# A mixture-of-experts / attention kernel: the second stage's tokens are routed in four batches, most of them inside the attention

## The reference

```python
x = x + 0.5 * ffn(layernorm(x))
x = x + attn(layernorm(x), keys, values)     # 16 heads of 8, 512 keys; attn adds its own input
x = x + 0.5 * ffn(layernorm(x))
# ffn(z): xn = layernorm(z) * scale + bias; probs = softmax(xn @ gate.T)
#         the two best of 8 experts, their weights normalised to a sum of 1
#         out = swiglu(z; shared) + sum over the two of weight * swiglu(z; expert)
# swiglu: 128 -> 256 (gate, up) -> 128
```

## Time and profile before

| | us |
|---|---|
| median of 3 runs | 976.35 (974.88 to 979.6) |
| the profiled execution, its own time | 977.33 |
| its span, first to last instruction | 975.3 |
| first stage's routing, keys, scatters (0 to 129) | 129 |
| its 39 tiles (129 to 250) | 121 |
| results added (250 to 273) | 23 |
| attention with its start (273 to 701) | 428 |
| second stage: routing to its first tile (701 to 827) | 126 |
| its 39 tiles, results, stores (827 to 975.3) | 148 |

### The profile page before, as it was taken

How to read it: one execution, slowest core, us unless ns; L and a number is a source line. 1 busy time by engine, 2 the same in 40 slices (tenths; PEclk the granted TensorE clock), 3 DMA queues, 4 the chain that set the end, 5 groups by cost and what they waited for, 6 DMA issues and landing times.

```text
span 975.3 us, 13685 instructions
## 1 busy us (share of the span) xinstructions
PE 719.5 (74%) x4404; PEld 431.9 (44%) x4404; DVE 567.0 (58%) x1092; ACT 475.3 (49%) x733; POOL 530.2 (54%) x664
## 2 busy tenths in 40 slices
PE   4459669999026888888888888888645970999950
PEld 4325459999012333333333333333144540899950
DVE  5753324444327788888888888888348330444424
ACT  2232135555002677777777777777612210555530
POOL 5587726677151535464645464642175775466760
PEclk9859979999555799999999999999955995999985
DMA  8231123332400000000000000000000311333317
GB/s 235 84 97 59 60 75 98 91 96 64 151 22 0 1 7 19 7 19 7 20 7 19 7 19 8 19 7 20 14 11 32 107 61 63 88 91 91 99 54 232
DMA packets 57227, 55.09 MB, mean 56 GB/s; under 512 B 12828, under 2 KB 46367, under 8 KB 57158
## 3 DMA queue, kind: packets, MB, share of 16 engines
q1 hardware_dynamic: 48070, 36.38, 13.1%
q0 software_dynamic: 9088, 17.86, 5.1%
HBM read 29.13 MB, written 24.53 MB: 55 GB/s over the span
## 4 chain that ended last, share of the span: by engine, by line
PE 50%; POOL 19%; issue 9%; DVE 9%; ACT 7%; DMA 5%; SPq 1%; POOLq 0%; ACTq 0%; DVEq 0%
POOL slot_rows L1025 13%; PE psum L580 11%; PE psum L540 8%; PE psum L504 7%; PE psum L463 7%; PE psum L472 7%; ACT probs L687 6%; DVE neg_max L963 5%; PE psum L551 4%; PE psum L370 3%; DMA ycomb<-result_rows 3%; PE psum L396 1%; POOL a_z L1089 1%; POOL q_first L1098 1%; POOL rstd L1004 1%
## 5 line engine op out<-in xcount | busy, mean ns | idle before, releaser
L963 DVE TENSOR_REDUCE neg_max<-psum 128x1 f32<-128x512 f32 x512 | 329.0, 685 | 76.7 <-PE psum L551 68.0
L687 ACT ACTIVATE probs<-psum 128x1024 f32<-128x1024 f32 x256 | 255.7, 1024 | 80.7 <-PE psum L540 74.0
L918 DVE TENSOR_TENSOR work<-work,psum 128x512 f32<-128x512 f32 x110 | 74.4, 687 | 191.3 <-PE psum L472 133.3
L551 PE MATMUL psum<-k_stack,q_parts 32*128 32x512 f32 x512 | 133.8, 517 | 46.1 <-DVE neg_max L963 42.8
L1025 POOL DMA_INDIRECT slot_rows<-zrow,slot x128 | 127.3, 995 | 54.5 <-issue 45.8
L580 PE MATMUL psum<-probs,v_pad 128*32 128x512 f32 x1024 | 139.6, 618 | 0.2
L540 PE MATMUL psum<-q_full,k_stack 32*128 32x512 f32 x512 | 116.7, 479 | 17.6 <-ACT probs L687 17.6
L1044 POOL DMA_INDIRECT result_rows<-yrow,zslot x80 | 82.0, 1025 | 59.6 <-ACT yrow L661 30.2
L540 PEld LDWEIGHTS psum<-q_full,k_stack 32*128 32x128 f32 x512 | 48.2, 186 | 145.3 <-ACT probs L687 88.1
L648 ACT ACTIVATE work<-psum 128x512 f32<-128x512 f32 x110 | 65.7, 597 | 88.2 <-PE psum L457 66.3
L1044 POOL DMA_INDIRECT result_rows<-yrow,probs x76 | 77.1, 1014 | 30.0 <-issue 28.1
(11 more groups left out here) (160 smaller groups left out, 948.0 us busy)
## 6 DMA issues: line engine op xcount, KB each, us to landing
ycomb<-result_rows SPq DMA_DIRECT2D x32, 256.0 KB, 2.9
zslot<-slot_rows SPq DMA_DIRECT2D x40, 144.0 KB, 2.3
probs<-slot_rows SPq DMA_DIRECT2D x38, 144.0 KB, 2.3
slot_rows<-padrow SPq DMA_DIRECT2D x17, 144.0 KB, 1.9
x<-in_x SPq DMA_DIRECT2D x8, 256.0 KB, 4.0
slot_rows<-zrow,slot POOLq DMA_INDIRECT x128, 2.3
ycomb<-ycomb SPq DMA_DIRECT2D x64, 32.0 KB, 1.9
ycomb<-recip SPq DMA_DIRECT2D x32, 64.0 KB
```

Source lines behind the costliest of these rows:

```text
L551: mm(bank(M_BANK[m % 3]), q_parts[rows, u % 2, qt * P:(qt + 1) * P], k_stack[rows, u % HI, :], start=True, stop=True).then_inc(m_filled, 1)
L687: nc.scalar.activation(probs[:, k % PRING, 2 * jp:2 * jp + 2, :], psum[:, b:b + 2, :], ACT.Exp, scale=float(DH) ** -0.5).then_inc(s_freed, 1)
L918: tt(h[:, k % 2, :], silu[:, k % 2, :], bank(U_BANK[k % 2]), ALU.mult).then_inc(h_ready, 1)
L963: reduce(neg_max[:, u % 2, qt, j:j + 1], bank(M_BANK[m % 3]), AX.X, ALU.max, negate=True).then_inc(m_freed, 1)
```

## The change

- **Batches.** The first stage is routed in four batches of two groups, the second in batches of groups 0 to 3, 4 and 5, 6, and 7. Normalising moves from DVE to ACT (one ACTIVATE with a scale and a bias per tile, L764 goes). Logits and positions are copied from PSUM by ACT; their banks come from the attention's ring.
- **Second stage inside the attention.** Moments of group g are taken three steps after POST(g). For the first two batches, variance, deviations, normalising, transposes, logits, routing (one of its steps behind each M) and the scatters of 24 of the 32 tiles (one tile, two DMAs, per step) are put beside the steps; the scatters from step 93 on for the first batch, from step 123 on for the second.
- **Tail.** Groups 6 and 7 are routed and scattered between the groups of the shared expert, whose work now stands in the lists `first` and `second`. As `zT` the second stage uses free buffers, so SP waits for the last gate and up product before it loads a tile.
- **Results of the first stage.** Groups 0 and 1 are added ahead of the attention, group g+2 at step 12 of group g. `ycomb` lies in `zrow`, in pieces of 512 B. In the second stage loads and stores alternate.
- **PROJ.** ACT makes both `q_round` and `q_first` from PSUM; POOL only subtracts.
- **POOL.** Its set-up stands ahead of the first deviations; one power per batch in place of one per group.

```diff
-BG = 4
-NBATCH = NG // BG
-BT = BG * GT
+BATCHES = tuple((ph, groups) for ph, of in enumerate((((0, 1), (2, 3), (4, 5), (6, 7)), ((0, 1, 2, 3), (4, 5), (6,), (7,))))
+                for groups in of)
+PER_PHASE = len(BATCHES) // 2
+BT = 4 * GT
+NTT = NG * GT
 RT = 27
-TB = 15
+TB = 14
...
+        def zT_of(ph, g):
+
+            if ph == 0:
+                return zT[:, g, :]
+            if g < 4:
+                return w_now[:].rearrange("p a c -> p (a c)")[:, g * GTOK:(g + 1) * GTOK]
+            if g < 6:
+                return zslot[:].rearrange("p a b c -> p (a b c)")[:, (g - 4) * GTOK:(g - 3) * GTOK]
+            return zslot_T[:].rearrange("p a n -> p (a n)") if g == 6 else probs[:, 0, 0, :]
+
+        def ycomb(r, k):
+
+            at = NTT // 2 + (2 * (r % 2) + k) * GT
+            return zrow[:, 1, at:at + GT, 0:H]
...
+        def front(n):
+
+            return [("BV", n), ("BR", n), ("BZ", n)] + [("ZT",) + (BATCHES[n][0], g) for g in BATCHES[n][1]] + [("BD", n), ("LG", n)]
+
+        def moments(n):
+            return [("BM", BATCHES[n][0], g) for g in BATCHES[n][1]]
+
+        def routed(n, parts=(0, 1)):
+            return ([("R", n)] * 15 + [("EX", n), ("POS", n)] if 0 in parts else []) + ([("R", n)] * 12 if 1 in parts else [])
+
+        def scatters(n):
+            return [("SC", n, tau) for tau in range(tiles_of(n).start, tiles_of(n).stop)]
+
+        def shared(g):
+            return [("GU", 2 * g), ("GU", 2 * g + 1)] + ([("DS", g - 1)] if g else [])
+
+        first = moments(0) + front(0)[:2] + moments(1) + front(1)[:2] + front(0)[2:] + routed(0, (0,)) + moments(2) + front(2)[:2]
+        first += routed(0, (1,)) + scatters(0) + front(1)[2:] + routed(1, (0,)) + moments(3) + front(3)[:2] + routed(1, (1,)) + scatters(1)
+        for n in (2, 3):
+            first += front(n)[2:] + routed(n) + (scatters(n) if n == 2 else [])
+        first += [("CNT", 0), ("TAB", 0)] + scatters(3) + [("KEYS",)]
+        for g in range(NG):
+            first += shared(g)
+        first += [("DS", NG - 1)]
...
+        beside = {k: [] for k in range(NG * PER_GROUP)}
+        between = {k: [] for k in range(NG * PER_GROUP)}
+
+        def posted(g):
+            return PER_GROUP * (g + 1) + AT["POST"]
+
+        for g in range(NG - 1):
+            beside[posted(g) + 3].append(("BM", 1, g))
+        for n in (PER_PHASE, PER_PHASE + 1):
+            groups = BATCHES[n][1]
+            k0 = posted(groups[-1])
+            beside[k0 + 3] += [("BV", n)]
+            beside[k0 + 4] += [("BR", n)]
+            beside[k0 + 6] += [("BZ", n)]
+            for m, g in enumerate(groups):
+                beside[k0 + 7 + m].append(("ZT", 1, g))
+            k = k0 + 7 + len(groups)
+            beside[k] += [("BD", n), ("LG", n)]
+            for m in range(15):
+                between[k + 1 + m // 4].append(("R", n))
+            beside[k + 4] += [("EX", n), ("POS", n)]
+            for m in range(12):
+                between[k + 6 + m // 4].append(("R", n))
+            for m, ev in enumerate(scatters(n)):
+                beside[min(k + 9 + m, NG * PER_GROUP - 1)].append(ev)
...
+            m = []
+            for n, ev in enumerate(maxima(k + M_LEAD)):
+                m += [[ev] + between[k][n:n + 1]]
+            if not m:
+                m = [between[k], [], [], []]
+            out = [("S", k, 0)] + m[0] + m[1]
             out += [("AV", k - AV_LAG)] if k >= AV_LAG else []
             if k % (2 * KB) == AV_LAG - 1 and k > AV_LAG:
                 out += [("EVAC", k // (2 * KB) - 1)]
-            out += [("S", k, 1)] + m[2:]
+            out += [("S", k, 1)] + m[2] + m[3]
...
+            if r == AT["CB"] and g + 2 < NG:
+                out += [("CB", g + 2)]
...
+            return out + beside[k]
+
+        attention = [("CB", 0), ("MOM", 0), ("LN", 0), ("CB", 1), ("Z", 0), ("YT", 0), ("PROJ", 0), ("PROJ", 1)]
+        attention += maxima(0) + maxima(1) + maxima(2) + maxima(3) + [("MT", 0), ("PROJ", 2)] + maxima(4) + maxima(5)
+        attention += [e for k in range(NG * PER_GROUP) for e in step_events(k)]
+        attention += [("AV", NG * PER_GROUP - n) for n in range(AV_LAG, 0, -1)] + [("EVAC", 2 * NG - 1)]
+
+        m, n = len(BATCHES) - 2, len(BATCHES) - 1
+        second = front(m) + [("RECIP", NG - 1)] + shared(0) + routed(m, (0,)) + shared(1) + routed(m, (1,)) + [("POST", NG - 1)] + shared(2)
+        second += moments(n) + front(n) + shared(3) + scatters(m) + routed(n, (0,)) + [("CNT", 1)] + shared(4) + routed(n, (1,)) + [("TAB", 1)]
+        second += scatters(n)
+        for g in range(5, NG):
+            second += shared(g)
+        second += [("DS", NG - 1)]
+        events = first + attention + second
...
+                else:
+                    sp.wait_ge(up_ready, STEPS + 2 * NG)
...
+            def load_results(ph, g):
+                if g >= 2:
+                    sp.wait_ge(combined, ph * NG + g - 1)
+                for k in range(2):
+                    sp.dma_start(ycomb(g, k), d["yd"][(k * NG + g) * GTOK:(k * NG + g + 1) * GTOK].rearrange("(p t) f -> p t f", t=GT)
+                                 ).then_inc(comb_in[g % 2], 16)
...
+            for g in range(4):
+                load_results(0, g)
             for g in range(NG):
                 place(g)
-            sp.wait_ge(x_attended, NG)
+                if g + 4 < NG:
+                    load_results(0, g + 4)
             ffn(1)
+            for g in range(2):
+                load_results(1, g)
             for g in range(NG):
+                if g + 2 < NG:
+                    load_results(1, g + 2)
...
+            def logits(n):
+                ph, groups = BATCHES[n]
+                pe.wait_ge(s_freed, use_of["ZT", ph, groups[-1]] + 1)
+                b = claim(use_of["LG", n])
+                for m in range(len(groups) * GT):
+                    last = mm(psum[:, b, m * NE:(m + 1) * NE], zT_of(ph, groups[m // GT])[:, (m % GT) * P:(m % GT + 1) * P],
+                              gate_s[:, 0, :], start=True, stop=True)
+                last.then_inc(s_filled, 1)
...
+            def gate_up(ph, k):
+
+                g, i = divmod(k, 2)
+                if k == 0:
+                    pe.wait_ge(in_w[0], 48)
+                    if ph == 0:
+                        pe.wait_ge(v_ready, 1)
+                    else:
+                        pe.wait_ge(m_freed, len(max_of))
+                        pe.wait_ge(s_freed, use_of["S", NK - 1, 1] + 1)
+                if i == 0:
+                    pe.wait_ge(s_freed, use_of["ZT", ph, g] + 1)
+                if k >= 2:
+                    pe.wait_ge(silu_ready, ph * STEPS + k - 1)
...
+            def normalise(n):
+                ph, groups = BATCHES[n]
+                act.wait_ge(shift_done, n + 1)
+                if ph:
+                    act.wait_ge(dispatched, LANDED)
+                for g in groups:
+                    for t in range(GT):
+                        tau = g * GT + t
+                        last = nc.scalar.activation(zrow[:, 0, tau, 0:H], token_tile(x, tau), ACT.Identity,
+                                                    bias=shift[:, tau:tau + 1], scale=rstd[:, tau:tau + 1])
+                    last.then_inc(z_done, 1)
+
+            def double_z(n):
+                ph, groups = BATCHES[n]
+                act.wait_ge(z_done, ph * NG + groups[-1] + 1)
+                if ph and groups[-1] >= NG // 2:
+                    act.wait_ge(combined, NG)
+                nc.scalar.copy(zrow[:, 1, tiles_of(n), 0:H], zrow[:, 0, tiles_of(n), 0:H]).then_inc(z_doubled, 1)
...
-                        if u:
-                            act.wait_ge(q_ready, u)
-                        nc.scalar.activation(q_fp[:], bank(b), ACT.Relu, bias=bq[:, i:i + 1]).then_inc(s_freed, 1)
+                        if u >= 2:
+                            act.wait_ge(q_ready, u - 1)
+                        nc.scalar.activation(q_round[:, u % 2, :], bank(b), ACT.Relu, bias=bq[:, i:i + 1]).then_inc(q_rounded, 1)
+                        nc.scalar.activation(q_first[:, u % 2, :], bank(b), ACT.Relu, bias=bq_first[:, i:i + 1],
+                                             scale=first_row).then_inc(s_freed, 1)
...
+            def combine(ph, g):
+                xg = x[:, g, :].rearrange("p (t f) -> p t f", t=GT)
+                dve.wait_ge(comb_in[g % 2], (ph * (NG // 2) + g // 2 + 1) * 32)
+                if g == 0:
+                    dve.wait_ge(shared_added, (ph + 1) * NG)
+                tt(xg, xg, ycomb(g, 0), ALU.add).then_inc(comb_half, 1)
+                dve.wait_ge(comb_half, ph * NG + g + 1)
+                tt(xg, xg, ycomb(g, 1), ALU.add).then_inc(combined, 1)
...
+            scale_gates()
+            run_stage(0, first)
             ffn(0)
-            attend()
-            prepare(1)
+            run(attention)
+            run_stage(1, second)
             ffn(1)
+            for g in range(NG):
+                combine(1, g)
...
```

(42 more changed lines are left out.)

747 lines of the change are left out of this document (368 added, 379 removed).

## The result

The changed kernel takes 997.21 us (992.73 to 1013.29) against 976.59 (974.88 to 979.60): ratio 1.0179, 95% interval 1.0142 to 1.0217. Forecast were 967 and a range of 944 to 984. Its executions spread more than those of before. The ratio is that of the three shorter ones, and the profiled one is the longest, 1013.29, 16.1 us above the median. The same program profiled once more (first experiment) gave 1008.87 and the same picture; its median was 1000.82.

A forecast was written before the change was run, and what follows sets the result against it. No engine was taken to bound the whole: DVE and PE alternate in the attention, POOL bounds the seam before the tiles. Terms -18.4 + 45.3 - 41.6 + 5 - 0.5 = -10.2 on 977.33 gave 967 us, range 944 to 984.

The forecast's parts named there:

- Start of the attention: From the first stage to the attention: first moments 16.7 us earlier, 1.7 saved in PROJ; -18.4 us.
- First stage: Before the attention: POOL's later start and deviations behind scatters delay the first tile; +5 us, bounds 0 to 9.
- The attention: All attention groups: work added on DVE, PE, ACT and POOL, less a saved wait; +45.3 us, 5.7 per group.
- Additions and moments: DVE in the attention: six combinations of 8.4 us and seven moments of 5.6 us, charged at 83%.
- Routing steps: DVE in the attention: 54 routing operations, 11.3 us, charged at 83%.
- Normalising: ACT in the attention: 24 tiles in pieces of 5.8 and 2.9 us, PE and DVE going on for 1.5; 7.2 us.
- Scatters: POOL in the attention: tiles of two DMAs, 2.53 us each, exceed POOL's room; +6.5 us, bounds 0 to 25.
- The clock as a rival: Tail: PE stays at 1.2 GHz between pauses, half the shared expert's products cold, +14; 981 us, chance 0.12.
- The tail: From the attention's end to the second stage's first tile: 85 us (bounds 76 and 105) against 126.6; -41.6 us.
- The end: Second stage's stores issued between loads, saving most issues after the last addition; -0.5 us, bounds -4 and +4.
- nothing on balance: Shared expert waits for group 6 and becomes the tail; tail 90, attention 50, time 977 us; chance 0.12.
- POOL becomes the limit: Attention: scatters delay the maxima's stage, PE stands in MT, some 40 us show rather than 6.5; 988 us, chance 0.17.

The follow-up runs named there:

- first experiment: The changed kernel itself, run and profiled once more without any edit; median 1000.82 us, ratio 1.0227.
- run 7: Run 4's kernel with only the 24 tiles' scatters moved from the attention to the start of the tail; ratio 1.0043.
- run 15: Reordered tail and first stage, logits and dense routing of groups 0 to 3 inside the attention; their 16 tiles' scatters moved inside too; 952.88 us, ratio 0.9741.
- run 5: Run 4's kernel with two tiles normalised per step, row copies and logits one group at a time, positions one step later; ratio 0.9827.
- run 2: The kernel before plus ten extra bn_stats in one piece on DVE at the end of step 12 of each attention group; 998.65 us, ratio 1.0224.
- Run 4: The changed kernel with each addition of results in its own step and moments taken one tile at a time; 982.13 us, ratio 1.0066.
- Run 14: Reordered kernel with logits and routing of groups 0 to 3 inside the attention, one routing step per attention step instead of four; 963.21 us, ratio 0.9858.
- run 8: The program of run 6 repeated on a chip where the kernel before took 977.33 us; 973.83 us, ratio 0.9965.
- run 6: Run 4's kernel with all second-stage routing moved to the tail, only additions and moments left in the attention; ratio 0.9953.

## Why the prediction was wrong

- **Start of the attention, -18.4:** right. From the first tile to the moments it is 17.7 us less, against 16.7 worked out. Of the 1.7 for PROJ 0.5 shows: from the moments to the first product with `q_parts` 15.5 us instead of 16.0. (The 256 given as a sign left out the later start of +5 in the same forecast; it was 264.19.)
- **First stage, +5 (0 to 9):** right in kind, but 9.7 is over the bound. The keys begin at 70.83 against 68.5, the first tile is at 138.9 against 136.7, and the 2.2 taken off for a warm start and overlap do not show.
- **The attention, +45.3:** the step that failed; +71.7 to +74.8 in the profiled executions. These are 8.1 and 16.1 us above their medians; with all of that taken off the attention it is about 59 to 64, an estimate from the same numbers. The sum charged each engine's added work by its amount. The terms had the wrong size in both directions, and one was missing: PE's clock after a piece.
  - Additions and moments, 14.0 us at 83%: 11.6. With PROJ's second activation (1.0) and the saved wait for a_z (-5) that makes 7.6 forecast. Together in one step they cost 20.6 (19.3 + 1.3), apart 1.3. The -5 was right: seven such waits of about 1 us before, one of 2.14 in after.
  - Routing steps 11.3 at 83% and positions 3.0, for 24 tiles: on 16 tiles, 1.9.
  - Transposes and logits, 8.7: 6.8 in pieces of a group.
  - Normalising, 7.2: in pieces of 8 tiles up to 19.1 more than one tile per step, which costs 3 to 9.
  - Scatters, +6.5 (0 to 25): 9.4 for 24 tiles (run 7), 13.2 for 16 (run 15).

  1.9 + 6.8 + 19.1 + 9.4 are 37 of the 51.1 that routing costs inside, and 3 for normalising at all makes 40. They come from different kernels and from one execution each, so this is an account and not a proof. The rest was not isolated; run 5, with two tiles normalised per step and pieces of one group, was no shorter, so it isn't the size of the pieces alone.
- **The clock as a rival:** right mechanism, wrong place. I looked for it in the tail, where rows of before showed it, and gave the attention a whole clock throughout, because it had one while DVE and PE were evenly fed. Even there it was not quite whole: at two of PE's waits for a_z, of 0.95 and 0.97 us, it fell in the trace of before, and these two units took 13.9 us where four others at the same place of a group took 12.5.

```profile
381.50:384.70 3.20, 3.20 (x16) 1.21 (x16) 1.66 (x3) 1.61 (x2) 1.76 (x4) 0.50 0.17 63
```

- **The tail, -41.6:** 95.2 against 85 (bounds 76 to 105; over 95 was named as a sign of being wrong). The shared expert starts at 783.33, 16.0 after T0 (15.5 worked out). The pauses I listed are there (4.04, 6.93, 5.33, 2.27: 18.6 us; the 19.9 worked out hold some work of PE besides). What I had as three restarts at 0.7 is a granted clock of 0.77 over the tail. No drain shows behind the table loads of after either: the one at 92.07 takes 1.28 us, and ACT's next operation starts at 93.36.

  The Trainium skill ("TensorE: Matmul & The Clock Gate", Part 1: The HAM clock gate) has the clock set by how busy the array has been recently, and the windows above agree, in the tail and in the attention. I had cited it for the tail only, and as a rule for an idle array. In the attention PE was not idle: it was busy 3.00 of 5.00 us in after and 2.29 of 4.00 in run 2, with no wait over 1.37, and the clock fell.
- **The end, -0.5:** +0.8, within its bounds.
- **The rivals:** "nothing on balance" had the right form (work moved behind an engine that is then the bound) with 50 us of attention and 90 of tail; both were exceeded. Run 4, without the pieces of additions and moments, is close to it: 52.4 and 93.0, ratio 1.0066. "POOL becomes the limit" did not decide here: PE's waits for `max_stage` in after are three, 4.3 us in all, none over 2.0. Its 988 is also a slip: 40 in place of 6.5 makes 967 into 1000.5. That this is near the measured 997.21 is chance, as the mechanism was not at work.

## What to carry over

Into a loop whose engines feed each other within a few microseconds, put work by the size of its pieces: 20 us of DVE work in pieces of 0.28 cost 2.8 us, 16 us in pieces of 2 cost 22 to 27. Run 14 warns that thin work alone is no guarantee. Price a piece by what the fed engine loses behind it, clock included, and look in the trace of before for a place where that engine went short of work, however short. Moving the results' additions into the loop was worth it. Routing as it stood there was not worth its 51 us, though 16 tiles' routing steps in small pieces cost 1.9 and saved 11.8 of tail; with the pieces apart and the tail reordered, four versions lie at 0.974 to 0.978 of the kernel before (951 to 957 us), and between them the measurement does not decide.

## What the runs showed of the hardware

- In run 4 the two additions of a group stand beside POOL's work, and take 1.63 and 1.11 us instead of the 0.68 and 0.69 above (POOL runs L1260, two inputs, from 423.25 to 424.53, and L1275 from 435.44 to 436.72):

```profile
423.44 1.63 DVE L1075 TENSOR_TENSOR x<-x,zrow 128x512 f32<-128x512 f32 x1
436.16 1.11 DVE L1078 TENSOR_TENSOR x<-x,zrow 128x512 f32<-128x512 f32 x1
```

The Trainium skill ("SBUF — State Buffer", Who interferes with whom) has a VectorE instruction with two SBUF inputs contend with a GpSimd instruction that reads SBUF. The rows agree; no run tested it by itself, and whatever it costs is within the 1.3 us of run 8, whose additions stand at the same places.

- On one chip the kernel before took 1080.53 us and all three of mine about as much more. Units inside the attention had the same 11.9 to 12.9 us there; stretches outside it did not: the first tile came at 175.99 (138.54 in run 8). In run 6 VectorE starts a routing step whose inputs are there 17.28 us late:

```profile
802.37 0.25 DVE L906 TENSOR_TENSOR r_a<-logits,rstd 128x32 f32<-128x32 f32 x1 [17.28 <-issue]
```

The same program took 973.83 us elsewhere, without such gaps. What the engine waits for there the profile doesn't show.
